# Beta and k's inverse norm multiplied in with the causal mask, head by head, in place of scaling v on GpSimd

## The reference

```
qn, kn = q / max(|q|, eps), k / max(|k|, eps)
gv     = beta[..., None] * v                     # beta = softplus(h @ b_w.T + b_b)
attn   = qn @ kn.T                               # i: query row, j: key row
out    = (attn * mask) @ gv                      # mask[i, j] = 1 for j <= i in the chunk as this kernel has it
```

## Time and profile before

| | us |
|---|---|
| median of 3 runs | 2280.11 (2276.76 to 2282.71) |
| the profiled execution's own time | 2278.17 |
| its span, first to last instruction | 2276.4 |
| TensorE busy in the span | 2194.5 |
| VectorE busy | 1176.5 |
| ScalarE busy | 1028.7 |
| GpSimd busy | 536.7 |
| mean granted TensorE clock | 0.988 of full speed |

### The profile page before, as it was taken

One profiled execution on the slowest core, in us unless ns is written; L12 is line 12 of the kernel. 1 busy time (PEld: TensorE's weight loads), 2 busy tenths in 40 slices (PEclk: granted clock), 3 DMA queues, 4 the chain that ended last, 5 costly groups with the idle time before them and its releaser, 6 DMA issues.

```text
span 2276.4 us, 34008 instructions
## 1 busy us (share of the span) xinstructions
PE 2194.5 (96%) x11420; PEld 1851.2 (81%) x11420; DVE 1176.5 (52%) x2171; ACT 1028.7 (45%) x3268; POOL 536.7 (24%) x540
## 2 busy tenths in 40 slices
PE   7999999999999999999999999999999999999998
PEld 6788778787878887877888888788888888888887
DVE  4555555455545554554554444555555545545554
ACT  4555555555555555555455454233433232233332
POOL 1334334333433343433343343000000000000000
PEclk9999999999999999999999999999999999999999
DMA  8454352353543534532322330253334223423221
GB/s 296 144 187 143 121 158 52 130 161 80 151 128 91 167 89 157 150 128 82 112 60 95 107 121 29 84 190 101 108 116 162 97 98 104 162 96 115 97 97 61
DMA packets 191885, 274.66 MB, mean 121 GB/s; under 512 B 99185, under 2 KB 132961, under 8 KB 191713
## 3 DMA queue, kind: packets, MB, share of 16 engines
q1 hardware_dynamic: 191712, 272.49, 37.4%
HBM read 214.79 MB, written 57.67 MB: 120 GB/s over the span
## 4 chain that ended last, share of the span: by engine, by line
PE 77%; DVE 4%; ACT 3%; issue 3%; DVEq 0%; ACTq 0%
PE proj_ps L634 39%; PE out_ps L634 12%; PE s_ps L831 4%; PE av_ps L840 4%; PE s_ps L883 3%; PE av_ps L883 3%; PE qt_ps L883 3%; PE kt_ps L883 3%; PE qt_ps L817 2%; PE kt_ps L822 1%; PE misc_ps L659 1%; ACT gated_hi L1050 1%; DVE gated L1353 1%; ACT squares L1042 1%; PE misc_ps L697 1%
## 5 line engine op out<-in xcount | busy, mean ns | idle before, releaser
L634 PE MATMUL proj_ps<-w_qkv,h_t 128*128 128x512 f32 x2304 | 623.0, 409 | 14.0 <-DVE q_sb L1332 5.8
L634 PEld LDWEIGHTS proj_ps<-w_qkv,h_t 128*128 128x128 f32 x2304 | 416.7, 192 | 97.4 <-issue 15.8
L634 PE MATMUL proj_ps<-h_t,w_qkv 128*128 128x512 f32 x1800 | 443.8, 391 | 0.0
L590 POOL TENSOR_TENSOR inv_norm<-guarded,minus_half 128x8 f32<-128x8 f32 x128 | 209.4, 1636 | 815.4 <-DVE guarded L1345 815.4
L634 PEld LDWEIGHTS proj_ps<-h_t,w_qkv 128*128 128x128 f32 x1800 | 336.1, 188 | 68.7
L1033 ACT ACTIVATE q_t<-qt_ps 128x512 f32<-128x512 f32 x128 | 76.3, 596 | 336.4 <-PE qt_ps L817 336.4
L634 PE MATMUL proj_ps<-h_t,w_gate 128*128 128x512 f32 x768 | 198.1, 411 | 27.1 <-ACT gate L1056 23.4
L1332 DVE TENSOR_TENSOR q_sb<-proj_ps,bias 128x512 f32<-128x512 f32 x128 | 88.4, 690 | 218.2 <-PE proj_ps L634 204.2
L634 PEld LDWEIGHTS proj_ps<-h_t,w_gate 128*128 128x128 f32 x768 | 145.2, 195 | 66.6 <-ACT gate L1056 31.2
L1042 ACT ACTIVATE squares<-q_sb 128x128 f32<-128x128 f32 x512 | 151.5, 298 | 58.2 <-DVE q_sb L1332 52.8
L1042 ACT ACTIVATE squares<-k_sb 128x128 f32<-128x128 f32 x512 | 151.6, 297 | 45.3 <-DVE k_sb L1332 43.3
(11 more groups left out here) (193 smaller groups left out, 3232.0 us busy)
## 6 DMA issues: line engine op xcount, KB each, us to landing
w_qkv<-tile_scr SPq DMA_DIRECT2D x100, 768.0 KB, 4.3
w_qkv<-head_scr SPq DMA_DIRECT2D x45, 1024.0 KB, 11.5
head_scr<-stage SPq DMA_DIRECT2D x30, 512.0 KB, 3.1
w_gate<-head_scr SPq DMA_DIRECT2D x15, 1024.0 KB, 4.9
w_out<-head_scr SPq DMA_DIRECT2D x15, 1024.0 KB, 6.0
tile_scr<-stage SPq DMA_DIRECT2D x25, 512.0 KB, 3.4
x_in<-_attn_hidden_states_dram SPq DMA_DIRECT2D x16, 512.0 KB, 7.7
h_scr<-stage SPq DMA_DIRECT2D x16, 512.0 KB, 3.0
```

The source lines that it names most:

```text
L590: pool.tensor_tensor(inv_norm[b][:, :], guarded[b][:, :], minus_half[:, :], ALU.pow).then_inc(inverted, 1)
L634: mm = pe.matmul(out, w, y, start=(j == 0 and m == 0), stop=(3 * j + m == n - 1))
```

## The change

GpSimd no longer scales v; its other three instructions stay. The mask becomes four VectorE instructions, one for each head, each multiplying 128 columns of `s_ps` by a scalar for each partition (that head's column of `v_scale`) and by `causal`. The semaphore `v_scaled` is gone: `attend` waits for the biased v, `mask` waits for `v_scale`, and GpSimd waits for the mask before it writes `v_scale` again.

```
@@ gpsimd, in step n
-                after(pool, v_scaled, n - 1)
+                after(pool, masked, n - 1)
                 pool.wait_ge(beta_ready, s + 1)
                 pool.tensor_tensor(v_scale[b][:, :], inv_norm[b][:, HG:2 * HG],
                                    beta[:, s * TS + t, g * HG:(g + 1) * HG], ALU.mult).then_inc(scale_done, 1)
-                pool.wait_ge(scale_done, n + 1)
-                pool.wait_ge(biased[V], n + 1)
-                v = heads(raw[V][b][:, :])
-                pool.tensor_tensor(v, v, v_scale[b][:, :].unsqueeze(2).broadcast_to([P, HG, P]), ALU.mult)\
-                    .then_inc(v_scaled, 1)
@@ tensor, attend(n)
                 pe.wait_ge(masked, n)
-                pe.wait_ge(v_scaled, n)
+                pe.wait_ge(biased[V], n)
@@ vector, mask(n)
                 dve.wait_ge(scored, n)
                 after(dve, attended, n - 1)
-                dve.tensor_tensor(heads(scores[:, :]), heads(s_ps[:, :]),
-                                  causal[:, :].unsqueeze(1).broadcast_to([P, HG, P]), ALU.mult).then_inc(masked, 1)
+                dve.wait_ge(scale_done, n)
+                for h in range(HG):
+                    at = slice(h * P, (h + 1) * P)
+                    m = dve.scalar_tensor_tensor(out=scores[:, at], in0=s_ps[:, at], scalar=v_scale[(n - 1) % 2][:, h:h + 1],
+                                                 in1=causal[:, :], op0=ALU.mult, op1=ALU.mult)
+                m.then_inc(masked, 1)
```

More of the change, by code:

```diff
@@ L237, in build @@
                                                               sem("guard_done"), sem("inverted"))
-        q_scaled, scale_done, v_scaled = sem("q_scaled"), sem("v_scale_done"), sem("v_scaled")
+        q_scaled, scale_done = sem("q_scaled"), sem("v_scale_done")
         q_turned, k_turned, qt_copied, kt_copied = sem("q_turned"), sem("k_turned"), sem("qt_copied"), sem("kt_copied")
```

## The result

The changed kernel takes 2292.85 us in the median of four runs (2289.08 to 2297.8), the kernel before 2280.1 on the same chip (2276.76 to 2282.71): a ratio of 1.0052, with an interval of 1.0032 to 1.0073. Repeated later beside 11 runs of before (2280.84), five runs gave 2292.02 and 1.0051 [1.0037, 1.0065]. The change costs about 12 us. The execution profiled has 2289.08 us of its own and a span of 2287.3, so 10.9 more than that of before.

A forecast was written before the change was run, and what follows sets the result against it. TensorE was taken to bound the kernel, other engines counting only where their results reach it late. 5.6 + 7.1 + 0.7 + 1 = 14.4 us took the median from 2280.11 to 2294.5; own range 2288 to 2303, over all 2282 to 2312.

The forecast's parts named there:

- The mask grows by 0.42: VectorE's mask: four pieces with a scalar take 1113 ns where one instruction took 690, so 0.42 us more.
- the lower bound of 0.24: Growth of the mask in us if the scalar costs nothing: four pieces in 928 ns.
- Rival 1: At the mask: the scalar is free, growth 0.24, time 2284, no change to be told; chance 0.17.
- rival 2: At the mask: four pieces don't overlap or delays run in series, growth 0.68, time 2318; chance 0.15 for above 2303.
- The rule of the Trainium skill: Price of VectorE's pieces: about 75 ns per instruction, so the mask grows 0.225 us and the sum is 4 us.
- 70 masks with lead, 0.08 each, 5.6 us: At attend: growth 0.42 exceeds the 0.34 lead of 70 masks, costing 0.08 us each, 5.6 in all.
- The lead: How much the mask can grow before TensorE shifts behind attend: 0.34 us (1.28 - 0.94) at 70 masks.
- Masks without lead, 0.42 each: At 23 masks TensorE already waits for: 17 cost 0.42 us each, 7.1; six behind line 1152 cost 0.12, 0.7.
- this chain at 1 us: VectorE's work behind the mask comes up to 0.42 later; 1 us added for places where this cancels less well.
- Removal of line 602: Without GpSimd's scaling of v, a shorter line 1152 brings six late masks forward by about 0.3 us each.
- Rival 3: Lines 1361 and 1152: faster, as VectorE no longer meets line 602; 21.2 us back against 14.4, time 2273; chance 0.05.
- Nothing for the waits moved, v_scale and the experts: Moved waits of mask, GpSimd and attend cost nothing, v_scale being written 6.49 us before; experts' stretch as long as before.

The follow-up runs named there:

- experiment 1: The kernel before with its mask cut into four 128-column multiplications without a scalar, GpSimd still scaling v: 2287.47 against 2281.4 us, 1.0021.
- experiment 2: The kernel before with its mask as four instructions with a column of ones as scalar, GpSimd still scaling v: 2301.05 against 2281.4 us, 1.0085.
- experiment 4: The changed kernel with a semaphore step for each of the four pieces, attend waiting for each head's own: 2286.63 against 2281.4 us for before, 1.0016.
- experiment 3: The kernel before without GpSimd's scaling of v, mask as it was, result lacking beta and k's inverse norm: 2275.35 against 2281.4 us, 0.9971.
- experiment 7: The changed kernel with lo_part (line 1361) moved from VectorE to GpSimd: 2289.12 against 2279.42 us for before, 1.0048.
- experiment 8: The changed kernel with a signal for each piece and lo_part moved to GpSimd: 2281.26 us, ratio to before 1.0003.
- experiment 5: The kernel before with its mask in four pieces without scalar, a signal for each, GpSimd still scaling v: 2284.57 against 2279.42 us, 1.0026.
- experiment 6: The kernel before with its mask in two pieces of two heads, without scalar, a signal for each: 2280.31 us, ratio to before 1.0002.
- experiment 10: The kernel before with GpSimd's scaling of v moved one step later, in front of the power, mask unchanged: 2270.26 against 2280.84 us, 0.9954.

## Why the prediction was right

The forecast was 2294.5 us and +0.63%; 2292.85 and +0.52% were measured, so the total is 1.6 us off. Two of its terms were each off by more, in opposite directions, so that the total came this near is luck in part.

- **The mask grows by 0.42.** 0.44 was measured (1.13 against 0.69); 343 ns for a piece where 342 was forecast. The choice of line 1381 as the nearest row was right because both of its features cost: experiment 1 gives a growth of 0.19 without the scalar, below the lower bound of 0.24. Rival 1, the free scalar, is excluded by experiment 2, and rival 2, no overlap, by the 1.13. That the 61 ns are the scalar's, and not the operation's, is borne out by the same operation with a constant as scalar: `soft` at line 1184, 128x64 from SBUF, takes 214 ns, and the tensor_tensor of the same shape at line 1189 takes 225.
- **The rule of the Trainium skill** (Vector Engine (DVE) Microarchitecture Reference, Measured stream behaviour on trn2), some 75 ns for each further instruction, is near for the pieces without scalar: 0.19 us for three of them is 63 ns each. It doesn't fit those with a scalar from memory, where 0.44 gives 147.
- **70 masks with lead, 0.08 each, 5.6 us.** 54 of the steps behind these masks grew, by 0.12 in the mean and 0.13 in the quiet steps, 6.3 us in all. The lead was 0.31 rather than 0.34: with growth 0.44 the start of the loads moved by 0.13. Of the other 16 steps 13 became shorter (2.9 us), 12 of them those of experiment 2. With line 602 in place (experiment 2) ten of the 70 cost some 0.43 and not 0.08: a lead before `attend` doesn't help where TensorE's next wait is for what VectorE does behind the mask. The forecast had no such class. The waits for `attend` came out as said, 97 of them where some 90 were forecast. The quiet four steps have 38.34 where the text has 38.2.
- **Masks without lead, 0.42 each.** 23 of them, before the help for six, make 9.7 us. 21 steps grew by 0.43 in the mean, 9.0 us. 17 of them are behind masks of this class, four behind others, and two more of the class lie in steps whose clock changed. The price was right and the number came near, but the reason wasn't whole. I counted the cost at `attend`; experiment 4 takes that wait away and the cost stays, because the chain behind the mask on VectorE is just as late. The text had set this chain at 1 us, as a thing that cancels.
- **Removal of line 602.** I let it help six masks behind line 1152, by 0.3 each. The six moved, by 0.24 to 0.5 and one by 0.84, but six more stand behind `var_eps`, of which the forecast says nothing. Experiment 3 gives 5.1 us in its steps and 6.6 in its ratio (3.9 to 9.1 by its interval), where the forecast has 1.8; with the long mask the removal gives 7.5 in 12 steps. This is the term that was mis-sized most. The reading that failed was to look for contention only at instructions of 512 columns with two SBUF inputs. A count in it is off too: line 602 alone overlaps line 1361 at 40 places, with a mean of 0.89 us, not at 26 with 1.0. Rival 3 was right that removal gives time, and wrong that it could outweigh the mask.
- **Nothing for the waits moved, v_scale and the experts.** As said: no wait for v_scale shows, and the experts' stretch has the same busy time.

So the total came out near because two misses cancel: the dearer mask costs 19.6 us by experiment 2 (13.7 to 25 by its interval), where the forecast has 5.6 + 9.7 + 1 = 16.3, and the removal gives 6.6 by experiment 3, where it has 1.8.

What stays open: the parts of experiment 3's 6.6 us that no step shows, the lower clock in the steps of masks 53 and 85, and how much of the 85 us of VectorE that `lo_part` on GpSimd frees is lost to `var_eps` and the split of the input (1068 ns in the mean in experiment 7, 689 in the change). Rows of experiment 8 name the waits that remain, but not what delays each.

## What to carry to other kernels

Where an engine waits for another in nearly every step, a change of 0.1 us at that place counts by the number of steps: compare the growth of the instruction with the distance to the first wait behind it, and treat the steps where the instruction is already late, or where the next wait is for the work behind it, as a class of their own, in which the whole queue pays. Before work is moved off GpSimd onto a busier engine, try to move it in time: the same instruction one step later, against work that reads PSUM or against a wait, gave 10.6 us here (5.8 of it in 18 steps other than those of masks 100 and 108), while getting rid of it at the price of a longer mask lost 12. And when looking for what a GpSimd instruction holds up, look at the small VectorE instructions beside it too, each in the timeline and not by its group's mean: most keep their time, but one that is held up passes its whole delay on to what stands behind it.

## What the hardware showed beyond that

**Behind the same wait of 1.01 us TensorE's clock fell in one execution and not in the other.** The same place, mask 66, in before: the window (the clock is the third column from the end) and the timeline.

```profile
768.50:783.00 14.50, 13.49 (x75) 11.66 (x74) 4.59 (x8) 5.08 (x16) 3.88 (x4) 0.88 0.60 231
```

```profile
777.11 2.24 PE L659 MATMUL misc_ps<-gate_wt,h_f 128*128 128x16 f32 x16 [1.01 <-ACTq L959]
...
779.20 2.91 PE L634 MATMUL proj_ps<-w_qkv,h_t 128*128 128x512 f32 x6
```

And in after:

```profile
773.00:786.00 13.00, 11.99 (x76) 10.44 (x75) 5.07 (x11) 5.00 (x16) 2.85 (x3) 1.00 0.62 220
```

```profile
781.77 1.93 PE L654 MATMUL misc_ps<-gate_wt,h_f 128*128 128x16 f32 x16 [1.01 <-ACTq L954]
...
783.55 1.63 PE L629 MATMUL proj_ps<-w_qkv,h_t 128*128 128x512 f32 x6
```

The wait is the same, but the six matmuls of the projection took 2.91 us in before and 1.63 in after. Granted 0.88 in the mean of the window, the clock was at its lower level of 1.2 GHz for part of it. This step is 1.58 us shorter in after, and owes nothing to the change: it is as short in the traces of experiments 1, 5, 6 and 10, which have the old work on GpSimd. The four runs of after with clocks of 0.989, 0.987, 0.987 and 0.985 took 2289.08, 2292.8, 2292.89 and 2297.8 us, so episodes of this kind are most of the spread. Why the clock falls at one such wait and not at the next, these runs don't show.

**GpSimd holds up some small VectorE instructions until its own ends.** 4 columns (`var_eps`) took 0.46 us instead of 0.17, 64 columns (`picked`) 1.10 instead of 0.22, each ending within 0.1 us of the GpSimd instruction. The one of four columns has a single SBUF input. Size doesn't decide it: beside line 602 in before, the aggregation of mean and variance (128x2) kept its 0.15 us, the sum `total` (128x4) its 0.22 and its reciprocal 0.18. The bias addition and the gate's product, which read PSUM, kept their 0.69 and 0.68 us beside the same GpSimd instruction. And `inv_norm`, 128x8 in 1.64 us, held up nothing here: `picked` took 0.22 beside it six times in experiment 10.

**Which of the two waits is settled by who starts first, within some nanoseconds.** `picked` and the scaling of q start together at 66 places of the 11 traces other than experiment 10's. Where GpSimd started 5 to 22 ns earlier (24 places), `picked` took 1.10 to 1.12 us and GpSimd 1.04; where it started at most 5 ns earlier, or later (42 places), `picked` took 0.22 and GpSimd 1.10 to 1.13. One of the second kind, in before, against the row at 1149.29 above:

```profile
440.05 1.13 POOL L593 TENSOR_TENSOR q_sb<-q_sb,inv_norm 128x512 f32<-128x512 f32 x1
440.05 0.23 DVE L1248 TENSOR_TENSOR picked<-picked,total 128x64 f32<-128x64 f32 x1
```

So a change that moves either engine by 0.02 us can win or lose 0.9 us at such a place, which has to be taken out before two kernels are compared.

**A scalar from SBUF costs a VectorE instruction 61 ns** (343 against 282 for 128 columns read from PSUM), and four pieces in a row pay it in full.
